# A planned order of work, laid out anew: the letter tables of a five-engine kernel

## The chip, the cores and the metric

The kernel runs on one core of a Trainium2 chip. A core has five engines with their own instruction queues: TensorE (PE in the profile, its weight loads PEld), VectorE (DVE), ScalarE (ACT), GpSimd (POOL) and SyncE (SP), which here issues all transfers between the device memory and the chip. The metric is the device time of one execution in microseconds; the kernel before took 2635.39 us as the median of three runs (2631.88 to 2636.12).

## The reference, cut to what matters

Four residual layers act on x of shape (8, 256, 64, 64), eight images of 256 channels. Each first normalises over 32 groups of channels:

```python
x = x + _L0_conv_ref(_gn(x), ...)   # three 7x7 gates over pooled (max, mean) planes, mixed by a softmax
x = x + _L1_conv_ref(_gn(x), ...)   # a 3x3 convolution, its weight mixed with block-circulant projections of itself
x = x + _L2_conv_ref(_gn(x), ...)   # a squeeze and excitation over channels (8-tap pairs folded into a weighted mean)
x = x + _L3_conv_ref(_gn(x), ...)   # shifted 8x8 window attention, 8 heads, with a relative bias and a mask
```

## The kernel before, in words

**Two lines of work.** Each image passes through a chain of named steps, the list FRONT (L508): `norm0a` to `norm0c` (group statistics of the first layer), `reduce0` to `reduce15` (channel maxima and means: TensorE turns two pairs of rows a step, L1986, VectorE takes their maxima, L1531), `zpool`, `hwconv` to `bandturn` (the three gates), `hwmean0` to `hwmean7`, `logits`, `mix`, `mixturn` (their mixture), `gate0` to `gate17` (the gated image, two matmuls a step on TensorE, L2058 and L2060, one product and one statistic on VectorE, L1624 and L1457), `norm1a` to `norm1c`, `lift0` to `lift3`, `conv0.0` to `conv23.1` (the convolution in a transformed form, 24 outputs of 18 matmuls, L2088) and `convend`. Beside it run streams of other work, one letter for each: on all engines `Y` is the setup of the weights in the first image and `E` the excitation; the attention of the image before, in 64 rows of windows, is `K` (tokens), `Q` (projections on TensorE, six matmuls of 512 columns each or twelve of 256, L2147, L2154 and L2163, and their evacuations on ScalarE), `S` (scores and maxima), `X` (exponentials), `T` (sums on VectorE, L1862 and L1864; turned probabilities on TensorE, L2189), `N` (normalisation on GpSimd), `W` on TensorE (the weighted values, L2208), `O` (heads) and `A` (the result added to the row on VectorE, L1871). For the image itself VectorE has `C` (statistics, L1727), `U` (maxima over rows and columns, L1742 and L1749), `B` and `J` (lower half of the convolution's inputs, and joined rows), `V` (row sums, L1713 and L1716); GpSimd has `R` (row and column sums), `D` (differences) and `W` (weighed rows, L902); SP has `Z` and `F` (store an image, fetch the next), `L` and `S` (load and store a row) and `G` (constants again).

**What sets the order.** An engine runs its queue in order. The queue is written out from tables: FIRST for the first image, TURN for each of the seven others, LAST_ROWS for the rows after the last image. An entry gives, for an engine and a step of the chain, the letters that are issued behind the engine's own part of that step (M). AHEAD names how many letters of a kind the first image has already done for the second; they are skipped there. The tables do not change what is computed, nor which semaphore an instruction waits for: an instruction that is issued too early stands in the queue and holds what is behind it.

```python
ahead, at_img = dict(AHEAD[engine]), 0
for kind, img, name in MAIN:
    ...
    yield "M"
    for letter in (TURN if at_img else FIRST)[engine].get(name, ""):
        if at_img == 1 and ahead.get(letter, 0):
            ahead[letter] -= 1
        else:
            yield letter
yield from LAST_ROWS[engine]
```

**Places that the prediction touches.** In the setup VectorE finds each partition's peak of the attention's weights (L1356 to L1358), GpSimd reduces them over partitions (L791 and L792), and VectorE scales by them (L1361 to L1369); each of the three is one `Y` of its engine. `norm0b` on VectorE writes the variance (L1446), GpSimd raises it to the power -1/2, `norm0c` on VectorE writes the shift (L1453), and ScalarE then normalises the first quarter of the image (L1082), for which `reduce0` on TensorE waits. A projection `p` (L2163) is added to the row by `A`; the next projection's bank is free when that is done. On SP the 64 transfers of the bias table (L671) are the last `Y`; the step `hwgate` has one transfer there (L689) and `hwrows` three (L693).

Of the kernel before, what the change touches and what calls it, by code (L numbers as in the profile page):

```python
# [7 lines left out]
NB, C, H, W = 8, 256, 64, 64  # L8
# [57 lines left out]
    "DVE": {"load": "YYUCUCCCCUCUCUCUCCCUCCUCYYYYYYYCC", "norm0a": "Y", "norm0b": "YYYY", "norm0c": "YYY",  # L66
# [7 lines left out]
        "convend": "JJJVCVVVVVVVCEUCUCCCUYUUUCEYAUACEEECCCCECECCEE"},  # L74
    "PE": {"reduce10": "Y", "reduce15": "Y", "zpool": "Y", "hwmean2": "Y", "hwmean5": "Y", "gate11": "Y",
        "gate17": "Y", "convend": "EYEEEEE"},
# [2234 lines left out]
```

How the kernel before makes its waits and increments, by code:

```python
            def link(self, ins):  # L444
                self.n += 1
                ins.then_inc(self.s, 1)
                self.eng.wait_ge(self.s, self.n)
# [88 lines left out]
        def wait_read(eng, name):  # L536
            if name in ADDED:
                eng.wait_ge(p_added, ADDED.index(name) + 1)
            elif name in BY_DVE:
                eng.wait_ge(v_taken, BY_DVE.index(name) + 1)
            else:
                eng.wait_ge(qp_read, BY_ACT.index(name) + 1)
# [75 lines left out]
                def load():  # L619
                    sp.dma_start(al[:, 0, :], dram(alphas, 0, [[0, P], [1, 5]])).then_inc(al_in, 16)
                    for u in range(UNITS):
                        half, co, ty, px = unit(u)
                        sp.dma_start(X[:, co, px], x[0, P * co:P * co + P, px]).then_inc(x_in[u], 16)
                    for dst, src in small:
                        sp.dma_start(dst, src).then_inc(consts_in, 16)
                    for g in range(P // BMAX):
                        sp.dma_start(WB[g::P // BMAX, :].rearrange("p (r n) -> p r n", r=BMAX),
                                     dram(w_conv, g * 2 * BMAX * TAPS, [[BMAX * C * TAPS, BMAX], [C * TAPS, BMAX],
                                                                        [1, 2 * BMAX * TAPS]])).then_inc(wconv_in, 16)
                    sp.wait_ge(zero_set, 1)
                    sp.dma_start(scratch_t[:, :], zeros).then_inc(zero_out, 16)
                    yield "load"
```

## Time and profile before

| | |
|---|---|
| median of three runs | 2635.39 us |
| profiled execution, its own time | 2639.28 us |
| its span | 2637.5 us |
| PE busy | 2268.7 us, 86% |
| DVE busy | 2210.3 us, 84% |
| ACT busy | 1550.4 us, 59% |
| POOL busy | 1445.6 us, 55% |
| mean granted TensorE clock | 0.956 |

A granted clock of 1.00 is 2.4 GHz and of 0.50 is 1.2 GHz. Busy time of PE counts matmuls from start to modelled end, so that one that stands alone counts longer than its share of a stream. Letters have no row of their own in the profile: a letter is found by the line that it issues. The convolutions of the eight images lie at 199.7, 490.1, 796.5, 1096.9, 1398.5, 1701.3, 2004.4 and 2307.1 us; the image that begins at 1264.8 us stands for the six between the second and the last, which are alike.

### The profile page before, as it was taken

What the parts mean: (1) busy time and instruction counts of PE and PEld (TensorE: products, weight loads), DVE (VectorE), ACT (ScalarE), POOL (GpSimd) and SP (SyncE); (2) the same over time, 40 slices, a digit from 0 to 9 for tenths busy, and PEclk for the clock granted to TensorE, in tenths of its full rate; (3) what the DMA queues carried; (4) which work ended last, traced back from release to release, by engine and by line L of the source; (5) the groups of instructions that cost most, each with busy time, mean ns of one, the idle gap of its engine ahead of it and who ended that gap; (6) DMA issues with size and microseconds to landing.
All of it is one profiled execution on the core that took longest, in us unless ns stands there. A gap on an engine that the chain in (4) does not pass through costs nothing. (4 is left out here: it accounts for less than half of the span.)

```text
span 2637.5 us, 67221 instructions
## 1 busy us (share of the span) xinstructions
PE 2268.7 (86%) x27686; PEld 1345.1 (51%) x27686; DVE 2210.3 (84%) x3721; ACT 1550.4 (59%) x3574; POOL 1445.6 (55%) x1150
## 2 busy tenths in 40 slices
PE   0558669898989989899989989899898989899897
PEld 0423346454745556455654557455664556545554
DVE  8988958888887988889898898879888888878665
ACT  1222046656765577645775567755766567755775
POOL 4315643466645583457735584466834676456455
PEclk9869879998999999999999999999999999999999
DMA  5400501022310231023311231104311223101221
GB/s 161 141 2 17 182 3 43 25 89 81 98 42 34 97 113 50 26 73 105 90 38 44 97 114 42 34 33 136 90 42 34 81 89 98 34 33 49 66 66 42
DMA packets 126065, 180.36 MB, mean 68 GB/s; under 512 B 72624, under 2 KB 114368, under 8 KB 115648
## 3 DMA queue, kind: packets, MB, share of 16 engines
q1 hardware_dynamic: 125760, 176.07, 21.3%
q8 instruction: 219, 3.59, 0.6%
q14 instruction: 86, 0.70, 0.1%
HBM read 103.15 MB, written 72.86 MB: 67 GB/s over the span
## 5 line engine op out<-in xcount | busy, mean ns | idle before, releaser
L2088 PE MATMUL F<-g_raw,cw_hi 128*128 128x512 f16 x2304 | 695.8, 384 | 17.5 <-DVE X L1497 8.7
L917 POOL TENSOR_TENSOR xs<-xs,rec 128x512 f32<-128x512 f32 x256 | 290.9, 1151 | 535.8 <-DVE rec L1864 534.5
L1206 ACT ACTIVATE xs<-xs,mx 128x64 f32<-128x64 f32 x1792 | 444.5, 334 | 40.3 <-DVE mx L1854 39.9
L2088 PE MATMUL F<-g_raw,cw_lo 128*128 128x512 f16 x1152 | 441.6, 383 | 0.0
L2088 PEld LDWEIGHTS F<-g_raw,cw_hi 128*128 128x128 f16 x2304 | 222.3, 98 | 282.3 <-issue 15.0
L1211 ACT ACTIVATE xs<-PTR 128x512 f32<-128x512 f32 x256 | 151.1, 590 | 214.8 <-PE PTR L2189 214.7
L902 POOL TENSOR_TENSOR tmp<-X,uw 128x512 f32<-128x512 f32 x128 | 175.9, 1391 | 130.7 <-DVE X L1699 93.4
L932 POOL TENSOR_TENSOR ot_lo<-ot,ot_hi 128x512 f16<-128x512 f32 x128 | 148.8, 1184 | 176.2 <-ACT ot_hi L1225 174.5
L1843 DVE TENSOR_TENSOR xs<-SP,bias 128x1024 f32<-128x1024 f32 (+2 forms) x192 | 159.8, 860 | 96.1 <-PE SP L2179 55.3
L1426 DVE SCALAR_TENSOR_TENSOR g_raw<-l0c,gn,g_raw 128x512 f16<-128x512 f32 x192 | 179.0, 975 | 51.6 <-ACT g_raw L1064 35.6
L2147 PE MATMUL QP<-tok_hi,qkv_hi 128*128 128x512 f16 x470 | 180.7, 385 | 34.6 <-ACT qq L1187 14.4
L1187 ACT ACTIVATE qq<-QP,q_bias,q_scale 128x512 f32<-128x512 f32 x118 | 91.6, 776 | 178.7 <-PE QP L2147 178.6
L1862 DVE TENSOR_REDUCE sums<-xs 128x16 f32<-128x1024 f32 x128 | 154.9, 1210 | 45.2 <-ACT xs L1201 24.1
L2088 PEld LDWEIGHTS F<-g_raw,cw_lo 128*128 128x128 f16 x1152 | 113.2, 98 | 141.0 <-issue 4.0
L2147 PE MATMUL QP<-tok_lo,qkv_hi 128*128 128x512 f16 x470 | 179.5, 382 | 0.0
L2189 PE MATMUL PTR<-ident,xs 128*128 128x128 f32 x1024 | 159.9, 279 | 22.8 <-ACT xs L1211 12.2
L2147 PE MATMUL QP<-tok_hi,qkv_lo 128*128 128x512 f16 x470 | 179.2, 381 | 0.0
L1986 PE MATMUL F<-ident,g_raw 128*128 128x129 f32 x1024 | 148.7, 290 | 35.0 <-ACT g_raw L1082 20.3
L1854 DVE TENSOR_REDUCE mx<-xs 128x16 f32<-128x1024 f32 x128 | 156.1, 1220 | 13.7
L2179 PE MATMUL SP<-kk,qq 32*64 32x64 f32 x8192 | 154.6, 224 | 11.2 <-issue 5.5
L1986 PEld LDWEIGHTS F<-ident,g_raw 128*128 128x128 f32 x1024 | 131.9, 198 | 55.6 <-DVE Z L1531 24.1
L2189 PEld LDWEIGHTS PTR<-ident,xs 128*128 128x128 f32 x1024 | 123.0, 143 | 68.7 <-POOL xs L917 31.9
(334 smaller groups left out, 5538.8 us busy)
## 6 DMA issues: line engine op xcount, KB each, us to landing
scratch_x<-X SPq DMA_DIRECT2D x32, 1024.0 KB, 4.8
xs<-scratch_x SPq DMA_DIRECT2D x56, 508.0 KB, 3.4
out_x<-xs SPq DMA_DIRECT2D x56, 508.0 KB, 2.8
X<-in_x SPq DMA_DIRECT2D x25, 1024.0 KB, 6.1
l0c<-scratch_t SPq DMA_DIRECT2D x8, 1876.0 KB, 9.0
l0c<-in_x SPq DMA_DIRECT2D x7, 1024.0 KB, 5.1
l0c<-scratch_t SPq DMA_DIRECT2D x8, 640.0 KB, 11.1
l0c<-scratch_t SPq DMA_DIRECT2D x8, 576.0 KB, 12.1
```

The source lines that it names most:

```text
L902: G.tensor_tensor(rows_view(tmp[:, 2 + m % 2, :]), rows_view(X[:, co, lo:lo + CHUNK]), uw[:, :].unsqueeze(1).to_broadcast([P, ROWS, W]), A ...
L917: G.tensor_tensor(keyed(sc[:, u % DEEP, :]), keyed(sc[:, u % DEEP, :]), rec[:, u % DEEP, :].unsqueeze(2).to_broadcast([P, 8, TOK]), ALU.mu ...
L1206: last = S.activation(keys, keys, ACT.Exp, bias=mx[:, u % DEEP, i:i + 1])
L1426: V.scalar_tensor_tensor(vin[:, slot(half, comp), 1, t, :, 1:1 + W], rows_view(src[:, t, :]), g_r[:, t:t + 1], vin[:, slot(half, comp), 0, ...
L1843: return V.tensor_tensor(windows(sc[:, buf:buf + 2, :])[:, :, w0:w1_, :], windows(SP[:, :, :])[:, :, w0:w1_, :], bias[:, kind, :, :, :].re ...
L1854: V.tensor_reduce(mx[:, buf:buf + 2, :].rearrange("p a k -> p (a k)"), sc[:, buf:buf + 2, :].rearrange("p a (k m) -> p (a k) m", m=TOK), A ...
L1862: seq.link(V.tensor_reduce(both(sums), sc[:, buf:buf + 2, :].rearrange("p a (k m) -> p (a k) m", m=TOK), AX.X, ALU.add))
L1986: last = T.matmul(turned_pair(j)[:, t, :], Gn[:, t, P * j:P * j + P], ident_mean[:, :], start=True, stop=True)
L2088: last = T.matmul(F[:, n % 2, :], wgt[:, ci, C3 * comp + dx, P * co:P * co + P], win[which], start=(ci == 0 and dx == 0 and j == 0), stop= ...
L2147: last = T.matmul(out_bank, wgt[:, ci, P * oc:P * oc + P], tk[:, ci, :], start=(j == 0), stop=(j == 5))
L2179: last = T.matmul(SP[TOK * h2:TOK * h2 + TOK, hs, 256 * cg + TOK * w:256 * cg + TOK * w + TOK], qq[rows, cg, win], kk[rows, cg, win], star ...
L2189: last = T.transpose(PTR[:, P * b:P * b + P], sc[:, u % DEEP, P * b:P * b + P], ident[:, :])
```

## The change

All five tables are written anew; no other line differs. The order that they hold was worked out with TensorE's stretches at half clock counted in their account. The number of letters of each kind in TURN is the same before and after. In FIRST, VectorE does two `U` and two `A` less (AHEAD gives 6 in place of 8, and 2 in place of 4), and ScalarE one `K` less (AHEAD gives none in place of 1). Cut to the rows that are spoken of below:

```diff
 FIRST = {
-    "SP": {"load": "YYY", "band2": "Y", "hwmean2": "Z", "gate0": "ZFF", "gate2": "F", "gate14": "Z", "norm1a": "F",
-        "conv4.1": "Z", "conv10.0": "L", "conv22.0": "L", "conv23.1": "S", "convend": "GL"},
...
-        "reduce12": "RR", "reduce15": "R", "band2": "R", "lift2": "D", "lift3": "D", "conv0.1": "D", "conv1.0": "D",
-        "conv5.1": "D", "conv6.0": "YD", "conv7.0": "W", "conv9.0": "W", "conv9.1": "W", "conv11.0": "W",
...
-    "DVE": {"load": "YYUCUCCCCUCUCUCUCCCUCCUCYYYYYYYCC", "norm0a": "Y", "norm0b": "YYYY", "norm0c": "YYY",
...
-        "bandcopy": "YY", "logits": "YY", "mix": "YY", "mixturn": "Y", "gate16": "Y", "norm1c": "Y", "conv3.1": "BY",
-        "conv6.1": "BBY", "conv8.0": "JB", "conv8.1": "JJB", "conv10.1": "VVBB", "conv11.0": "VB", "conv11.1": "V",
...
-        "convend": "JJJVCVVVVVVVCEUCUCCCUYUUUCEYAUACEEECCCCECECCEE"},
...
+    "SP": {"norm0a": "Y", "reduce3": "Y", "reduce11": "Y", "reduce13": "Y", "hwmean1": "ZF", "gate2": "Z",
+        "gate4": "F", "gate9": "F", "gate11": "Z", "lift2": "F", "lift3": "Z", "conv22.1": "SL", "conv23.1": "G",
+        "convend": "LL"},
...
+        "reduce14": "R", "reduce15": "RRR", "zpool": "R", "lift3": "D", "conv1.1": "DD", "conv2.1": "D",
+        "conv4.0": "Y", "conv5.0": "DW", "conv6.1": "W", "conv7.1": "W", "conv9.0": "DW", "conv13.0": "W",
...
+    "DVE": {"load": "YYCCCCCCUUUCCUCUCCCUCUCCCYYYYYYY", "norm0a": "YYYYYYYY", "norm0c": "Y", "reduce0": "U",
...
+        "mixturn": "Y", "gate1": "Y", "lift1": "Y", "conv4.0": "BY", "conv4.1": "B", "conv5.1": "BB", "conv6.0": "J",
+        "conv6.1": "B", "conv8.0": "JBJ", "conv8.1": "V", "conv9.0": "V", "conv9.1": "Y", "conv10.1": "VVV",
...
+        "conv22.1": "CVVCVVUUV", "conv23.0": "V", "convend": "JJJVVVVVVVVUCUUEUUYUUECEEECECECCCCCEE"},
...
 TURN = {
...
-    "DVE": {"norm0a": "E", "norm0b": "TA", "norm0c": "KKAU", "reduce1": "T", "reduce2": "U", "reduce3": "U",
...
-        "mixturn": "ATKA", "gate1": "K", "gate4": "T", "gate9": "S", "gate15": "SAKK", "gate16": "ATT", "lift1": "S",
...
-    "PE": {"norm0b": "Q", "norm0c": "QTQ", "reduce2": "Q", "reduce3": "Q", "reduce5": "TQ", "reduce6": "STWT",
-        "reduce7": "SQW", "reduce8": "Q", "reduce11": "Q", "reduce12": "T", "reduce13": "QT", "reduce14": "Q",
-        "zpool": "Q", "hwconv": "Q", "hwgate": "WTQTQWS", "hwrows": "Q", "band0": "S", "band2": "Q", "bandturn": "Q",
-        "hwmean0": "T", "hwmean1": "Q", "hwmean2": "TQW", "hwmean3": "Q", "hwmean4": "T", "hwmean5": "Q",
-        "hwmean6": "T", "hwmean7": "QWS", "logits": "S", "mix": "Q", "mixturn": "Q", "gate0": "Q", "gate1": "T",
-        "gate3": "Q", "gate4": "QT", "gate6": "QT", "gate8": "Q", "gate10": "SQTW", "gate12": "S", "gate14": "W",
-        "gate15": "QQ", "gate16": "QQQ", "gate17": "T", "norm1a": "Q", "lift0": "TQ", "lift1": "TQST", "lift2": "WW",
-        "conv0.1": "QSQ", "conv1.0": "Q", "conv2.1": "T", "conv7.0": "QT", "conv8.0": "Q", "conv9.0": "QT",
-        "conv9.1": "Q", "conv10.0": "WS", "conv10.1": "TQ", "conv11.0": "WS", "conv11.1": "Q", "conv13.0": "Q",
-        "conv15.0": "Q", "conv16.0": "Q", "conv16.1": "Q", "conv17.0": "TQ", "conv17.1": "QT", "conv19.0": "T",
-        "conv19.1": "WSQT", "conv20.0": "WS", "conv20.1": "Q", "conv22.0": "Q", "conv23.0": "Q", "conv23.1": "TQ",
-        "convend": "TQWTQTQEWEQEESQESE"},
+    "DVE": {"norm0a": "E", "norm0b": "U", "norm0c": "TAKUK", "reduce0": "A", "reduce1": "U", "reduce2": "U",
...
+        "band1": "S", "band3": "TAK", "bandturn": "A", "hwmean0": "T", "logits": "S", "mix": "ST", "mixturn": "A",
+        "gate1": "KKA", "gate3": "T", "gate9": "S", "gate12": "S", "gate15": "AK", "gate16": "KATT", "lift1": "S",
...
+    "PE": {"norm0b": "Q", "norm0c": "Q", "reduce1": "Q", "reduce2": "Q", "reduce3": "T", "reduce4": "QT",
+        "reduce5": "Q", "reduce6": "WST", "reduce7": "TQSW", "reduce8": "Q", "reduce11": "Q", "reduce12": "T",
+        "reduce13": "QT", "reduce14": "Q", "reduce15": "Q", "hwgate": "QWTQTQWS", "hwrows": "Q", "band0": "S",
+        "band3": "Q", "bandturn": "TQ", "hwmean1": "TQ", "hwmean2": "WQ", "hwmean3": "Q", "hwmean5": "TQ",
+        "hwmean6": "T", "hwmean7": "QWS", "logits": "S", "mix": "Q", "mixturn": "Q", "gate1": "QT", "gate3": "Q",
+        "gate5": "QT", "gate6": "Q", "gate8": "Q", "gate9": "ST", "gate11": "WQT", "gate12": "SW", "gate14": "Q",
+        "gate15": "Q", "gate17": "QQQ", "norm1a": "Q", "norm1b": "TT", "lift0": "QW", "lift2": "T", "lift3": "TSW",
+        "conv0.0": "Q", "conv0.1": "QSQ", "conv1.1": "Q", "conv2.1": "T", "conv6.1": "QT", "conv7.0": "Q",
+        "conv7.1": "Q", "conv9.0": "Q", "conv9.1": "TQTWS", "conv10.1": "WS", "conv12.0": "Q", "conv13.1": "Q",
+        "conv15.1": "Q", "conv16.1": "TQ", "conv17.0": "T", "conv17.1": "Q", "conv18.0": "TQ", "conv18.1": "Q",
+        "conv19.1": "WSQT", "conv20.0": "WS", "conv20.1": "Q", "conv22.0": "Q", "conv22.1": "Q", "conv23.1": "TQTQ",
+        "convend": "TQTWQEWEQEESQESE"},
...
-AHEAD = {"SP": {}, "POOL": {"N": 4, "O": 1, "R": 22}, "ACT": {"K": 1, "O": 1, "T": 4, "X": 2}, "DVE": {"A": 4, "E": 1, "T": 2, "U": 8}, "PE": {"Q": 2, "T": 4, "W": 2}}
+AHEAD = {"SP": {}, "POOL": {"N": 4, "O": 1, "R": 22}, "ACT": {"O": 1, "T": 4, "X": 2}, "DVE": {"A": 2, "E": 1, "T": 2, "U": 6}, "PE": {"Q": 2, "T": 4, "W": 2}}
...
```

## Rows read from the trace of the kernel before

**Rows 1.** One stretch: from:to, us, busy PE, PEld, DVE, ACT, POOL, clock, DMA.
```profile
199.70:306.80 107.10, 99.41 (x432) 42.97 (x432) 91.89 (x118) 22.47 (x35) 60.85 (x41) 0.96 0.17 59
```

**Rows 2.** Stretches of the image that begins at 1264.8 us.
```profile
1264.80:1350.60 85.80, 81.71 (x1292) 60.87 (x1291) 75.17 (x149) 64.68 (x151) 47.23 (x43) 0.98 0.27 80
1350.60:1398.50 47.90, 39.58 (x619) 21.49 (x619) 43.81 (x72) 34.29 (x87) 22.74 (x18) 1.00 0.15 46
1398.50:1533.90 135.40, 132.32 (x1190) 67.57 (x1187) 115.95 (x145) 73.64 (x178) 79.50 (x57) 1.00 0.19 63
1533.90:1566.80 32.90, 23.01 (x363) 14.54 (x362) 28.21 (x75) 23.05 (x55) 25.88 (x22) 0.90 0.33 103
```

**Rows 3.** TensorE in order of time around 1534 us: start, length, engine, line.
```profile
1533.73 0.60 PE L2189 MATMUL PTR<-ident,xs 128*128 128x128 f32 x4
1534.17 0.38 PE L2147 MATMUL QP<-tok_hi,qkv_hi 128*128 128x512 f16 x1
...
1535.46 0.60 PE L2189 MATMUL PTR<-ident,xs 128*128 128x128 f32 x4
```

**Rows 4.** VectorE in order of time around norm0.
```profile
1558.22 1.21 DVE L1862 TENSOR_REDUCE sums<-xs 128x16 f32<-128x1024 f32 x1
...
1560.68 0.75 DVE L1871 SCALAR_TENSOR_TENSOR xs<-QP,wm,xs 128x512 f32<-128x512 f32 x1 [0.90 <-PE QP L2163]
1561.35 0.15 DVE L1453 SCALAR_TENSOR_TENSOR gn<-F,gn 128x2 f32<-128x2 f32 x1
1561.42 3.33 DVE L1828 TENSOR_TENSOR tok_lo<-tok,tok_hi 128x512 f16<-128x512 f32 x2
...
1565.33 1.94 DVE L1749 TENSOR_REDUCE Z<-X 128x32 f32<-128x1024 f32 x1
```

**Rows 5.** TensorE in order of time around norm0.
```profile
1557.92 0.59 PE L2163 MATMUL QP<-ot_hi,wo_hi 128*128 128x512 f16 x1
...
1565.46 0.39 PE L2147 MATMUL QP<-tok_hi,qkv_hi 128*128 128x512 f16 x1 [2.07 <-DVE xs L1871]
...
1566.77 0.94 PE L1986 MATMUL F<-ident,g_raw 128*128 128x129 f32 x7
```

**Rows 6.** ScalarE in order of time around norm0.
```profile
1560.56 0.63 ACT L1172 ACTIVATE tok_hi<-tok 128x512 f16<-128x512 f32 x1
1561.54 2.38 ACT L1082 ACTIVATE g_raw<-X,gn 128x1024 f32<-128x1024 f32 x2 [0.34 <-DVE gn L1453]
```

**Rows 7.** GpSimd in order of time around norm0.
```profile
1559.09 0.70 POOL L836 TENSOR_TENSOR gn<-gn,neg_half 128x2 f32<-128x2 f32 x1
```

**Rows 8.** Stretches at half clock in two images.
```profile
1553.80:1560.60 6.80, 3.71 (x10) 1.66 (x10) 4.96 (x21) 6.10 (x21) 6.41 (x7) 0.50 0.00 0
1857.60:1867.80 10.20, 7.33 (x20) 3.29 (x20) 7.87 (x25) 9.14 (x24) 9.73 (x10) 0.50 0.00 0
```

**Rows 9.** GpSimd, VectorE and TensorE in order of time, first convolution.
```profile
239.21 0.41 POOL L791 PARTITION_ALL_REDUCE gm<-gm  x1 [5.85 <-issue]
...
240.00 0.15 DVE L1361 TENSOR_SCALAR gm<-gm 128x1 f32<-128x1 f32 x1 [4.36 <-POOL wm L792]
...
242.14 0.61 PE L2088 MATMUL F<-g_raw,cw_hi 128*128 128x512 f16 x2 [3.52 <-DVE X L1497]
```

**Rows 10.** SP in order of time, first image.
```profile
97.20 0.43 SPq L666 DMA_DIRECT2D ot<-in_w_qkv  x1
121.18 0.53 SPq L689 DMA_DIRECT2D tmp<-in_c_rows  x1
...
127.17 23.32 SPq L671 DMA_DIRECT2D tok_hi<-in_rel_t  x64
```

**Rows 11.** VectorE in order of time, between the first two images.
```profile
342.05 0.16 DVE L1774 SCALAR_TENSOR_TENSOR part<-F,part 128x2 f32<-128x2 f32 x1 [8.10 <-POOL part L912]
```

**Rows 12.** TensorE in order of time, second image's first steps.
```profile
356.60 0.61 PE L2147 MATMUL QP<-tok_hi,qkv_hi 128*128 128x512 f16 x1 [2.42 <-DVE tok_lo L1828]
...
359.13 4.86 PE L1986 MATMUL F<-ident,g_raw 128*128 128x129 f32 x24
```

More of the change, by code:

```diff
@@ L53 @@
 FIRST = {
[12 rows of a table removed]
-    "DVE": {"load": "YYUCUCCCCUCUCUCUCCCUCCUCYYYYYYYCC", "norm0a": "Y", "norm0b": "YYYY", "norm0c": "YYY",
[7 rows of a table removed]
-        "convend": "JJJVCVVVVVVVCEUCUCCCUYUUUCEYAUACEEECCCCECECCEE"},
-    "PE": {"reduce10": "Y", "reduce15": "Y", "zpool": "Y", "hwmean2": "Y", "hwmean5": "Y", "gate11": "Y",
-        "gate17": "Y", "convend": "EYEEEEE"},
[8 rows of a table added]
+        "convend": "WWRRRRRRRRRRRRRRRRERRRRRR"},
[14 rows of a table added]
 }
 TURN = {
[33 rows of a table removed]
-        "conv23.1": "KACV", "convend": "JJJVVVVVVVVECECEECESECESE"},
[11 rows of a table removed]
-        "convend": "TQWTQTQEWEQEESQESE"},
[23 rows of a table added]
+        "conv23.1": "XKXTQTQ", "convend": "TQKTQOEQQXX"},
[10 rows of a table added]
+        "convend": "JJJCVVVVVVVVECECEECESECESE"},
[11 rows of a table added]
+        "convend": "TQTWQEWEQEESQESE"},
 }
-AHEAD = {"SP": {}, "POOL": {"N": 4, "O": 1, "R": 22}, "ACT": {"K": 1, "O": 1, "T": 4, "X": 2}, "DVE": {"A": 4, "E": 1, "T": 2, "U": 8}, "PE": {"Q": 2, "T": 4, "W": 2}}
+AHEAD = {"SP": {}, "POOL": {"N": 4, "O": 1, "R": 22}, "ACT": {"O": 1, "T": 4, "X": 2}, "DVE": {"A": 2, "E": 1, "T": 2, "U": 6}, "PE": {"Q": 2, "T": 4, "W": 2}}
 LAST_ROWS = {
-    "SP": "SLSLSLSLSLLSSS",
-    "POOL": "ENNNNXOXXXNNNNXXOXNXNNNXXOXXNNNNXXOXNXNNNXXXONNXNNXXOXNXNNNXXNOXNXNNXXXXNNONNO",
-    "ACT": ("KKXXQTQTQQTKTKOKKXKXQQXXQQTTTKTOXXKKQXTXKQQTQTTKKOKXXXQQXKTQQTKTTKOXKXKXQQXTQQTTKTXOXKKXKTQQXTKQQTTO"
-          "XKXKQQXXQQTTTKXTXKOKKKQXQTXQQTTXXTXOXTKTTTO"),
-    "DVE": "EAKAKTTSPSKPKAATTSPSTKPKAATSKPPSKATATSPPKSKATATSSPTKPKAATSPPSKAKTATSTSPKPKAATSSTTTPAPASAA",
-    "PE": ("QQQQTQTQTWSTQWSQQQQQQQTQTSTWTWSQQQTQQQQTQTSTQWWSQQQQQTQTQTSTQWWSQQQQQTQTSWTSTWQQQQTQQQTQQTSTWWQSQQQQ"
-          "QQTSTTTSWWQQTQQQQQQTSWSTTWQTQTQTQTWWQQ"),
+    "SP": "SLSLSLSLSLSSSL",
+    "POOL": "ENNNNXOXXXNNNNXXOXXNNNNXXOXXNNNNXOXXXNNNNXXXONXNNNOXXXNXNNNXXNOXNXNNXXXXNNONNO",
+    "ACT": ("XKKTXQKTQQTQTKOKKXXQXQXKQTQTTTKXOKKXKKXQQXQTTQTTKOXXKKQXQXTQQTTKTKOKXXXQKQXQTQKTTTXXOKKXTXQQKQTQTKTK"
+          "OKXXXKQQQXQTTKTTXXOKKQXQXQTQTTXXTXOXTTKTTKO"),
+    "DVE": "AETAKKTSPSKPKAATTSPSKPKAATTSKPSPKATATSKPPSKATATSSTPPKKAATSKPPSKAATTSTPSKPKAATSSTPTTPAAASA",
+    "PE": ("QQTTQQQTQWTSQWSQQQQQQTQTSQTTWWSQQQQQQTQTQTSTQWWSQQQQQTQTQTSTQWWSQQQQQTQTSWTSTQWQQQTQQQTQTQTSQWWSQQQQ"
+          "QQTSTTWTQWSQTQQQQQQTSTWSQTWTQTQTQTWWQQ"),
 }
```

87 rows, old and new, of tables (FIRST, TURN) are left out of this document.

## The prediction

> **What bounds the kernel now.** I read the page's busy shares first. TensorE is busy 86% of the span and VectorE 84%, so neither bounds the whole, and the bound has to be found stage by stage. A table of busy time by stretch was therefore the second view. In the first image the convolution lasts 107.1 us with TensorE busy 99.41 us of it [rows 1]. Six images of some 302 us follow that are alike, and the one that begins at 1264.8 us falls into four stages [rows 2]: up to `mixturn` 85.8 us (TensorE 81.71, VectorE 75.17), the gated image 47.9 us (VectorE 43.81, TensorE 39.58), the convolution 135.4 us (TensorE 132.32, VectorE 115.95), and from its end to the next `reduce0` 32.9 us, in which nobody is full (VectorE 28.21, TensorE 23.01, clock 0.90). The reader is to see four bounds: TensorE in the first and the third stage, VectorE in the second, and a chain of waits in the fourth. A letter moved from one stage to another is worth something only by what bounds the two.
>
> The third view was the order of time around `norm0`, where the clock drops. The clock is at 0.50 for 6.8 us in one image and for 10.2 us in the next, under the same order [rows 8]. Before both, TensorE had long idle times: in the stretches shown it is busy 3.71 of 6.8 us and 7.33 of 10.2.
>
> **The change part by part.** All sums go against the profiled execution, 2639.28 us, 3.9 us above the median.
>
> *Prices.* A projection `Q` costs TensorE 1.29 us at full clock, from 1534.17 to the next group at 1535.46, and a `T` 0.44 us, from 1533.73 to 1534.17 [rows 3]. At half clock a projection that starts at 1557.92 lets VectorE go on at 1560.68, 2.76 us later [rows 4, 5]. On VectorE a `T` takes 1.56 us: it starts at 1558.22, and the wait of 0.90 us that follows it begins at 1559.78 [rows 4]. A `U` takes up to 1.94 us [rows 4].
>
> *norm0, in six boundaries.* VectorE now does `TA` behind the variance and the shift only then. `A` waits 0.90 us for the half-clock projection, so the shift comes at 1561.35 [rows 4], though GpSimd had the power ready at 1559.09 + 0.70 = 1559.79 [rows 7]. In the new table one `U` stands there: from 1558.22 it ends at 1560.16, and the shift is 1.2 us earlier. ScalarE is then still busy with tokens until 1561.19, so its normalisation starts not at 1561.54 but at 1561.2 at best [rows 6]: 0.3 us. More lies behind it. On TensorE two projections stand ahead of `reduce0`; the second is held 2.07 us by an `A` that VectorE does only after two `K` of 3.33 us, and `reduce0` starts at 1566.77, when its data have lain since 1561.54 + 2.38 = 1563.92 [rows 4 to 6]. The new table leaves one `Q` behind `norm0c` and has the other at `reduce1`. `reduce0` could then start at about 1563.7: −3.1 us. That is not all kept. From the end of the convolution to `norm0c` TensorE has two `Q` and two `T` less, of which one `Q` and one `T` come into the stage up to `mixturn`, which is full: 1.29 + 0.44 = +1.7 us. Sum −1.4 us an image. Bounds: 0, if the stage behind takes all of it back, and −2.9, if the 85.80 − 81.71 = 4.1 us of idle there hide all but a little.
>
> *The gated image, seven times.* VectorE bounds this stage and has one `T` less there (it now stands at `mix`): up to −1.5 us. TensorE has one `Q` less, which counts only where VectorE waits for it. I take −1.3, with 0 (the step waits for other engines) and −1.5 as ends. The `T` at `mix` lies in a stage where VectorE idles 85.80 − 75.17 = 10.6 us; if that cover is gone, it costs its 1.56 us there.
>
> *The convolution, seven times.* TensorE has two `Q` and one `T` more: 2 × 1.29 + 0.44 = +3.0 us in a stage with 135.40 − 132.32 = 3.1 us of idle [rows 2]. Much of this idle is the matmuls' waits for their inputs, which a letter fills only if it stands at the right place; I take +2.2, between 0 (all filled) and +3.0 (none). On VectorE one `C` leaves the stage, and 19 us of idle there cover the rest.
>
> *The first image's convolution.* VectorE stands 4.36 us until 240.00 for GpSimd's reduction over partitions, which GpSimd itself starts late (its 5.85 us idle with no releaser), and TensorE then stands 3.52 us until 242.14 [rows 9]. The new tables have VectorE's peaks and GpSimd's reduction at `conv4.0`, and the scales only at `conv9.1`, so the stall should go: −3.5. Ends: −4.4 (VectorE's whole stall) and +2, if the reduction now waits for VectorE's peaks and holds GpSimd's differences `D`, which stand behind it at `conv5.0`: no row shows that wait, and I bound it by half of today's 4.36.
>
> *Into the second image.* There a projection of six half-clock matmuls runs from 356.60 to 359.13, ahead of `reduce0` [rows 12]. It moves to `reduce1`. It ran while data were still on their way in part, so I take half, −1.3, between 0 and −2.5. Two `U` of up to 1.94 us come into this image's first steps on VectorE, where it waits for TensorE. Six `C` that leave `convend` gain nothing: VectorE stands 8.10 us there for GpSimd's excitation [rows 11], and GpSimd's letters ahead of that are not fewer.
>
> *At nothing.* The 64 transfers of the bias table take 23.32 us of SP's queue; they move ahead of the transfers of `hwgate` and `hwrows`, into a queue that issues nothing between 97.6 and 121.18 us [rows 10]; late by a little, they cost up to 2 us. The setup's reordering around `norm0a` lies beside weights that VectorE prepares anyway: 0, ±2. The fetches and `G` on SP, moved by some steps, lie beside a convolution of 135.4 us [rows 2]; if a fetch is late once, the longest wait in these rows, 8.10 us, bounds it [rows 11]. The rows after the last image have the same letters in a new order: 0, ±3.
>
> *Sum.* −3.5 − 1.3 + 6 × (−1.4) + 7 × (−1.3) + 7 × 2.2 = −3.5 − 1.3 − 8.4 − 9.1 + 15.4 = −6.9 us: 2639.3 becomes 2632.4 profiled, and on the median's scale 2635.4 − 6.9 = **2628 us**. With all lower ends the sum is −4.4 − 2.5 − 17.4 − 10.5 + 0 − 3, with the setup's −2 = −40; with all upper ends it is 2 + 0 + 0 + 0 + 21 + 2 + 2 + 3 = +30, and one late fetch more makes +38.
>
> The half-clock stretches differ by 3.4 us between images of one order [rows 8], about as much as the plan means to win at one boundary. The Trainium skill, "TensorE: Matmul & The Clock Gate", Part 1 (The HAM clock gate), says that how many matmuls run cold differs between runs of the same kernel. This speaks against any order built on fixed stretches, and the trace agrees so far as 6.8 and 10.2 us go; by that rule the −8.4 of the six boundaries may come to half or to nothing, the first rival below.
>
> **The rivals.**
>
> *No change, about 2634.* The stretches at half clock fall elsewhere under the new order, and a boundary gains in some images and loses in others. Then half of the six boundaries' −8.4 is kept (−4.2), the gated image keeps −9.1, the convolution costs its upper +3.0 (+21, less a third that the idle takes, +14), and the first image gives −4.8 only in part (−3): −2. For it: the 3.4 us above. Against it: `reduce0` waits at all six boundaries for the same `A`, at whichever clock.
>
> *Slower, about 2651.* The convolution is TensorE's, 132.32 of 135.40 us [rows 2]. If all 3.0 us come on top, seven images cost 21 us, and if neither the boundary nor the gated image gives anything back, because VectorE's letters set the pace there (43.81 of 47.9 us) and their whole count is the same, only the first image's −4.8 stands against it: +16. It decides from about 1.5 us an image that isn't given back. For it: the convolution is the one stage where a TensorE letter certainly costs. Against it: the letters are taken from stages in which TensorE was on the path too.
>
> *A larger gain, about 2600.* The idle of TensorE at each boundary, 32.9 − 23.01 = 9.9 us, shrinks by 5 and the idle in the convolution takes the added letters: 6 × (−5) − 5 = −35. For it: the 2.07 us wait and the half-clock projection are both in the chain. Against it: the sums of statistics and the excitation in that stage are a chain on VectorE and GpSimd, and it is not made shorter.
>
> *The order does not do what it says*, in that its half-clock stretches are as long as before: this changes no letter's place, and leads to the first rival's time.
>
> **How the numbers follow.** Chances: forecast 0.42, larger gain 0.08, no change 0.25, slower 0.25. A measurement of this kernel can tell 0.2%, about 5.3 us, from no change. The forecast at 2628 (−7) and the larger gain lie beyond it: faster 0.50. Within it: 0.25, slower 0.25. The forecast's own range, with the convolution between +1 and +2.7 an image and the boundary between −2.5 and −1, is 2618 to 2636. The range to hold the time 8 times in 10 reaches below to 2606, short of the larger gain's middle, and above to 2650, to the slower rival's middle: about 0.07 lies below and 0.13 above.
>
> **What would show it.** Right: at the six boundaries `reduce0` starts within some 2 us of its data, with no `A` wait of 2 us before a projection; the convolutions are 137 to 138 us long; the gated image is 46 to 47 us; and the first convolution shows no stall of VectorE near 240 us. Wrong in one step each: `reduce0` still 2.5 us behind its data; a convolution of 138.4 us or more, with TensorE's idle unchanged (slower); a stage up to `mixturn` longer by more than the 1.7 us. The whole is wrong if the period between `reduce0`s, 302 us, isn't shorter by about half a microsecond to one, or if the time moves in the setup or the rows at the end, which I cost at nothing.

## The result, and the profile after

The changed kernel takes 2619.17 us in the median of four runs (2613.57 to 2621.74), against 2635.76 us before: a ratio of 0.9931, 95% interval 0.9918 to 0.9945. That is −16.6 us where −7 were forecast, with the time inside the range. The profiled execution took 2613.57 us and the one of before 2639.28 us, so the two traces differ by 25.7 us: 3.5 us of that is how far the old trace lies over its median, and 5.6 how far the new one lies under its own.

The first view is the busy time by stretch, as in [rows 1, 2]: the first image's convolution, then the four stages of the image that begins at 950.60 us, whose period of 297.1 us is among the shorter ones (296.1 to 300.6). Columns are from:to, us, busy PE, PEld, DVE, ACT, POOL, granted clock, DMA share, GB/s. The program's lines are one further down than before.

```profile
203.70:303.00 99.30, 96.87 (x433) 42.42 (x434) 86.87 (x119) 19.91 (x31) 56.76 (x40) 0.98 0.19 64
950.60:1037.30 86.70, 82.98 (x1302) 61.52 (x1301) 76.82 (x152) 65.89 (x159) 50.31 (x47) 0.98 0.15 45
1037.30:1084.10 46.80, 37.75 (x606) 20.50 (x606) 42.72 (x71) 34.83 (x87) 21.36 (x17) 1.00 0.15 47
1084.10:1217.70 133.60, 133.37 (x1209) 68.79 (x1199) 116.98 (x144) 74.16 (x179) 81.73 (x57) 1.00 0.27 88
1217.70:1247.70 30.00, 21.03 (x353) 13.55 (x351) 26.61 (x75) 20.90 (x47) 23.67 (x21) 0.89 0.30 106
```

The row to see is the convolution: 133.60 us with TensorE busy 133.37. Before it was 135.40 with 132.32 [rows 2]. TensorE has 1.05 us more work in it and 2.85 us less idle time, so the stage with the added letters got shorter. What TensorE waited for there stands in the view of waits (engine, what, for whom: us in total, times, longest), first before, in the convolution from 1398.5 us:

```profile
PE O L2208 <- issue: 1.5, 1, 1.5
PE QP L2163 <- ACT vv L1194: 1.4, 1, 1.4
PE F L2088 <- DVE X L1497: 0.2, 1, 0.2
```

and in the changed kernel, in the one from 1084.1 us:

```profile
PE F L2089 <- DVE X L1498: 0.2, 1, 0.2
```

Of 3.1 us of waits, 2.9 belonged to two letters of the attention (a projection `Q` and a `W`) and only 0.2 to the convolution's own matmuls. Both big waits are gone. Over the seven convolutions the projection's wait for ScalarE is there in each before (0.8 to 1.4 us) and in one after (0.3 us).

Stage by stage the two traces add up so (image 0 is the first):

| part | before, us | after, us | difference | predicted |
|---|---|---|---|---|
| load to the second image's `reduce0` | 359.1 | 353.9 | −5.2 | −4.8 |
| `reduce0` to the gated image, images 1 to 7, sum | 603.4 | 607.7 | +4.3 | +10.2 |
| convolution's end to `reduce0`, six boundaries, sum | 195.6 | 184.2 | −11.4 | −18.6 |
| gated image, seven, sum | 334.1 | 330.5 | −3.7 | −9.1 |
| convolutions, seven, sum | 948.8 | 936.0 | −12.8 | +15.4 |
| last convolution's end to VectorE's last instruction | 192.9 | 195.9 | +3.0 | 0 |

(The predicted −3.1 at a boundary and +1.7 behind it are shown apart here, six times each. The first row flatters the change: one projection that stood ahead of the second image's `reduce0` now stands behind it, and that image's stage from `reduce0` to the gated image is 2.5 us longer, which the second row counts.)

At the boundary, in order of time around 1241 us (start, length, engine, line; the bracket is the wait before it), the new order looks so:

```profile
1241.80 1.91 DVE L1750 TENSOR_REDUCE Z<-X 128x32 f32<-128x1024 f32 x1
1244.11 0.16 DVE L1454 SCALAR_TENSOR_TENSOR gn<-F,gn 128x2 f32<-128x2 f32 x1 [0.40 <-POOL gn L837]
...
1244.69 2.36 ACT L1083 ACTIVATE g_raw<-X,gn 128x1024 f32<-128x1024 f32 x2
...
1243.38 0.70 POOL L837 TENSOR_TENSOR gn<-gn,neg_half 128x2 f32<-128x2 f32 x1
...
1246.42 0.39 PE L2164 MATMUL QP<-ot_hi,wo_hi 128*128 128x512 f16 x1 [2.18 <-DVE xs L1872]
...
1247.72 1.05 PE L1987 MATMUL F<-ident,g_raw 128*128 128x129 f32 x8
```

From the first letter behind the variance to the shift it is 2.31 us now (1241.80 to 1244.11) and was 3.13 [rows 4]: the `U` fills VectorE's wait, but GpSimd gives the power 2.28 us after that point (1243.38 + 0.70) in place of 1.57 [rows 4, 7]. `reduce0` starts 0.67 us behind its data (1244.69 + 2.36 = 1247.05), where it was 2.85 behind [rows 5, 6]. At the six boundaries `reduce0` starts 0.24 to 1.48 us behind its data, where it was 2.49 to 2.97. Yet a wait for VectorE's addition is still there at all six, of 1.75 to 2.18 us, only in front of the one projection that stayed.

In the first convolution the stall of VectorE is gone as foreseen [rows 9]; GpSimd reduces at 232.61, and VectorE's scales run at 245.96 with no wait. The second image's `reduce0` has no projection ahead of it [rows 12]:

```profile
232.61 0.42 POOL L792 PARTITION_ALL_REDUCE gm<-gm  x1 [5.73 <-issue]
...
245.96 0.14 DVE L1362 TENSOR_SCALAR gm<-gm 128x1 f32<-128x1 f32 x1
...
203.73 1.01 PE L2089 MATMUL F<-g_raw,cw_hi 128*128 128x512 f16 x2 [12.92 <-DVE cw_lo L1353]
...
353.89 2.33 PE L1987 MATMUL F<-ident,g_raw 128*128 128x129 f32 x9 [3.62 <-ACT g_raw L1083]
```

The third of these rows shows what the table hides: TensorE now stands 12.92 us before the first convolution for the weights that VectorE prepares (6.62 us for other data before), so of the 7.9 us by which that convolution is shorter, 6.0 are given back in the gated image ahead of it. Of these 7.9 us, 2.5 are TensorE's own work, which ran at a mean clock of 0.98 in place of 0.96 (99.41 to 96.87 us). The load is 5.8 us longer and the reduction 7.7 shorter in the same way.

### The profile page after: what moved, and what is told of

It reads as the page before. It is cut to its first block, busy times and chain, and to the rows that moved or that the text cites. A ratio compares the mean times of both kernels' runs of the same rounds, so it can differ in the third digit from the quotient of the medians.

```text
span 2611.8 us, 67227 instructions
## 1 busy us (share of the span) xinstructions
PE 2249.4 (86%) x27686; PEld 1342.5 (51%) x27686; DVE 2213.0 (85%) x3721; ACT 1548.9 (59%) x3574; POOL 1461.5 (56%) x1150
## 4 chain that ended last, share of the span: by engine, by line
PE 47%; DVE 21%; POOL 8%; ACT 7%; issue 5%; DMA 0%; DVEq 0%; POOLq 0%; SPq 0%; ACTq 0%
PE F L2089 23%; PE QP L2148 5%; POOL tmp L963 4%; PE QP L2155 3%; PE SP L2180 3%; ACT xs L1207 3%; PE PTR L2190 2%; PE O L2209 2%; PE F L1987 2%; PE QP L2164 2%; DVE sums L1863 2%; DVE xs L1844 1%; DVE mx L1855 1%; DVE raw L1572 1%; DVE stats L1458 1%
## 5 line engine op out<-in xcount | busy, mean ns | idle before, releaser
L903 POOL TENSOR_TENSOR tmp<-X,uw 128x512 f32<-128x512 f32 x128 | 168.8, 1336 | 122.5 <-DVE X L1700 119.2
L1427 DVE SCALAR_TENSOR_TENSOR g_raw<-l0c,gn,g_raw 128x512 f16<-128x512 f32 x192 | 159.4, 872 | 48.5 <-ACT g_raw L1065 38.5
L1191 ACT ACTIVATE kk<-QP,bq,gm 128x512 f32<-128x512 f32 x117 | 90.8, 776 | 144.2 <-PE QP L2148 144.0
L1987 PEld LDWEIGHTS F<-ident,g_raw 128*128 128x128 f32 x1024 | 133.5, 199 | 59.5 <-ACT g_raw L1083 31.7
```

Of the source, the lines that this page charges most:

```text
L903: G.tensor_tensor(rows_view(tmp[:, 2 + m % 2, :]), rows_view(X[:, co, lo:lo + CHUNK]), uw[:, :].unsqueeze(1).to_broadcast([P, ROWS, W]), A ...
L1427: V.scalar_tensor_tensor(vin[:, slot(half, comp), 1, t, :, 1:1 + W], rows_view(src[:, t, :]), g_r[:, t:t + 1], vin[:, slot(half, comp), 0, ...
L1987: last = T.matmul(turned_pair(j)[:, t, :], Gn[:, t, P * j:P * j + P], ident_mean[:, :], start=True, stop=True)
```

## The experiments

All ratios are to the kernel before, run on the same chip beside it; e1 to e4 shared one chip, e5 and a1 to a3 another, a0 and a4 to a6 a third.

| kernel | ratio | 95% interval | median, us |
|---|---|---|---|
| e1, new TURN alone | 0.9948 | 0.9929 to 0.9967 | 2620.6 |
| e2, norm0 alone | 1.0051 | 1.0031 to 1.0070 | 2648.4 |
| e3, one projection later | 1.0008 | 0.9996 to 1.0020 | 2637.6 |
| e4, SP's row alone | 0.9988 | 0.9976 to 1.0001 | 2632.8 |
| e5, new FIRST alone | 0.9987 | 0.9976 to 0.9997 | 2634.5 |
| a1, changed, old norm0 | 1.0013 | 0.9998 to 1.0027 | 2640.6 |
| a2, changed, TensorE kept busy | 1.0019 | 1.0006 to 1.0032 | 2643.0 |
| a3, changed, one more projection moved | 0.9982 | 0.9971 to 0.9994 | 2634.0 |
| a0, changed, again | 0.9945 | 0.9930 to 0.9961 | 2621.6 |
| a4, changed, old LAST_ROWS | 0.9947 | 0.9933 to 0.9960 | 2620.2 |
| a5, changed, old start of the convolution | 0.9933 | 0.9918 to 0.9948 | 2620.3 |
| a6, changed, one shift of 1.7 us | 0.9978 | 0.9967 to 0.9989 | 2628.9 |

**e1: which table holds the gain.** Before with the new TURN; FIRST, AHEAD and LAST_ROWS old.

> Before, with the new TURN alone; FIRST, AHEAD and LAST_ROWS are the old ones. Theory 1 (the first image gives a good quarter of the gain): in the profiles the first image and the way into the second are 5.2 us shorter and the rows at the end 3.0 us longer, so TURN alone would be worth 25.7 - 5.2 + 3.0 = 23.5 us between the two profiled runs, and about 14 us between medians, of which the six boundaries hold about 11, the seven gated images 4 and the convolutions 14, less some 4 in the stage up to mixturn. Theory 2 (the periods are shorter only because the first image hands over another state): under 5 us.

TURN alone gives −0.52%, nearly all of it, as theory 1 said. Its seven convolutions last 133.5 to 134.0 us, like the changed kernel's. But its periods come in two kinds: 296.0, 297.1 and 297.2 us, and 303.7, 303.9 and 303.5. Five of these periods (all but the 296.0 us of the second image) are one order, so the difference isn't the order's: the two short ones of 297 us hold 10.2 us at half clock, the three long ones 20.5 to 27.3. Two reductions of it, by stretch:

```profile
958.20:1044.90 86.70, 83.03 (x1302) 61.57 (x1300) 76.84 (x152) 65.68 (x159) 50.34 (x47) 0.98 0.16 45
1559.20:1648.20 89.00, 85.95 (x1302) 64.45 (x1300) 76.00 (x150) 64.60 (x158) 49.84 (x46) 0.94 0.15 44
```

The same 1302 matmuls take TensorE 2.92 us more in the second, at a mean clock of 0.94 in place of 0.98.

**e2: the boundary alone, in the old order.**

```diff
 TURN DVE
-"norm0b": "TA", "norm0c": "KKAU"
+"norm0b": "U", "norm0c": "TAKKA"
 TURN PE
-"norm0c": "QTQ"
+"norm0c": "Q", "reduce1": "TQ"
 TURN ACT
-"norm0b": "KK"
+"norm0c": "KK"
```

> Before, with the edits at norm0 alone: VectorE norm0b U and norm0c TAKKA in place of TA and KKAU, TensorE norm0c Q and reduce1 TQ in place of QTQ and nothing, ScalarE's KK behind norm0c in place of norm0b. Theory 1 (the boundary's chain was what held reduce0): from the convolution's end to reduce0 some 2.5 us less in each of six boundaries (32.6 becomes about 30), of which the projection and the turn that are moved into the stage behind take back 1.7 there: net -0.5 to -1.5 each, -3 to -9 us in all. Rival: the stage up to mixturn has 4 us of idle and takes them in, and all 2.5 are kept: -15 us. Second rival: the shift is late anyway, since GpSimd is still at its sums when the variance comes: under 1 us each.

The boundaries are 30.8 us long (one 31.0), 1.8 us less. The stage behind is 87.0 to 90.0 us long and was 83.0 to 88.1, which is more than was won (+18 us over seven against −11 over six), and the kernel is 0.5% slower; none of the three expected outcomes came. In the view by stretch, the stage up to `mixturn`, and the boundary behind that image:

```profile
1267.50:1355.60 88.10, 82.35 (x1303) 60.98 (x1302) 75.97 (x149) 64.97 (x153) 50.31 (x46) 1.00 0.27 80
1539.00:1570.00 31.00, 22.33 (x353) 13.90 (x352) 26.36 (x74) 22.48 (x54) 22.16 (x19) 0.81 0.32 104
```

This stage ran at full clock with 0.64 us more work on TensorE than in [rows 2], and yet lasts 2.3 us more: its idle time grew from 4.1 to 5.75 us. So the prediction's +1.7 for this stage is not a ceiling. Letters that arrive there make others wait.

**a1: the like edit undone in the new order.**

```diff
 TURN DVE
-"norm0b": "U", "norm0c": "TAKUK", "reduce0": "A", "reduce1": "U"
+"norm0b": "TA", "norm0c": "KKAU", "reduce1": "UU"
 TURN PE
-"norm0c": "Q", "reduce1": "Q"
+"norm0c": "QQ"
 TURN ACT
-"norm0c": "KK"
+"norm0b": "KK"
```

> The changed kernel with the old order at norm0: VectorE TA and KKAU, then UU at reduce1, TensorE QQ at norm0c and nothing at reduce1, ScalarE KK at norm0b. Theory 1 (what a boundary gains is taken back by the stage up to mixturn, as when norm0 alone was changed and the six images after it were no shorter): the boundaries are 2 us longer, the stage behind 1 to 2 us shorter, and the median is within 3 us of the changed kernel's 2619. Rival (in the new order the stage behind has room, and the boundary's 2.4 us are kept): +12 to +15 us, about 2632.

The rival came true. The shortest boundaries are 31.8 us against 30.0, the six in sum 199.1 against 184.2, and the stage behind is not shorter for it (607.4 us over seven against 607.7):

```profile
1226.40:1258.20 31.80, 22.48 (x359) 14.02 (x358) 27.89 (x76) 22.46 (x48) 25.47 (x21) 0.89 0.30 106
1258.20:1345.20 87.00, 80.80 (x1296) 59.80 (x1295) 77.05 (x151) 65.04 (x159) 48.49 (x46) 1.00 0.15 43
```

From 0.993 or 0.9945 the ratio rises to 1.0013, some 18 to 22 us. Between the traces, 18.7 us apart, the boundaries hold 14.9: 1.8 us at each of six make 11, and the rest lies at the three longest. The runs of this kernel scatter with the clock: their mean clock is 0.944 to 0.956, with 2648 us at the lowest and 2632 to 2636 at 0.953 to 0.956. Nearly the same edit is worth nothing, or less, in one order and all it gives at the boundary in the other. What in the new order makes the room was not isolated.

**e3 and a5: the wait of 1.4 us in the convolution.** e3 moves the waiting projection one step back in the old order; a5 puts the projections at the start of the new order's convolution back.

```diff
 e3, TURN PE
-"conv0.1": "QSQ", "conv1.0": "Q"
+"conv0.1": "QS", "conv1.0": "QQ"
 a5, TURN PE
-"lift3": "TSW", "conv0.0": "Q", "conv1.1": "Q"
+"lift3": "TSWQ", "conv1.0": "Q"
```

> Before, with one letter moved on TensorE: conv0.1 QS and conv1.0 QQ in place of QSQ and Q, so that the projection that stood 0.8 to 1.4 us for ScalarE's evacuation in each of seven convolutions comes one step later. Theory 1 (the convolution is TensorE's, and its idle time is added to it in full): each convolution 0.8 to 1.4 us shorter, -8 us in all, 0.3% under before. Rival (the idle is made up elsewhere, since the convolution's end waits for VectorE and GpSimd as well): the gap goes, the convolution keeps its 135 us, and the time is within 2 us of before.

> The changed kernel with TensorE's projections at the start of the convolution where they were: one back from conv0.0 to lift3 and one from conv1.1 to conv1.0, so that the last of QSQ at conv0.1 is early again. Theory 1 (in before this projection stood 0.8 to 1.4 us for ScalarE's evacuation behind its exponentials, and the new place took that stall out of every convolution): the gap before it is back with 0.8 us or more, and the convolutions become 134.5 to 135 us long in place of 133.6, +5 to +9 us in all. Rival (the stall went because ScalarE's own letters moved): no gap, 133.6 us as in the changed kernel, and the time within 2 us of it.

In e3 the wait did not go but change hands. In the convolution from 1700.8 us the projection now waits for VectorE's addition, and a matmul of the convolution for its input:

```profile
PE QP L2164 <- DVE xs L1872: 0.9, 1, 0.9
PE SP L2180 <- issue: 0.8, 1, 0.8
PE F L2089 <- DVE X L1498: 0.6, 1, 0.6
PE QP L2155 <- ACT vv L1195: 0.2, 1, 0.2
```

0.9 + 0.6 is as much as the 1.4 that went: the rival's idle time made up elsewhere is the nearer picture, and theory 1 failed. In a5 the wait for ScalarE's values did not come back at all: 132.06 us of work in convolutions of 132.3 us, one projection (1.3 us) less than in the changed kernel, and the time is that of the changed kernel. So TensorE's places at the start of the convolution are not what took the wait out; the rival names ScalarE's own letters, which the runs do not isolate.

**e4: transfers and the other wait.** SP's row of the new TURN in the old kernel.

> Before, with SP's row of the new TURN alone. In before, two image transfers of 1 MB are issued 0.6 us apart late in the convolution, the DMA share is 0.9 to 1.05 while they last, and TensorE stands 1.2 to 1.7 us at conv19 or conv20 in five of seven images with no releaser. Theory 1 (the stall is code that comes late past the transfers): with the transfers apart the stall goes, and the convolutions of these images are 1.2 to 1.7 us shorter, some -7 us in all. Rival (the stall belongs to the place in the code and not to the transfers): the stall stays at the same letters, and the time is within 2 us of before. Second rival: the transfers now collide with other code, and stalls of the same kind come up at another step.

In the kernel before, SP issues two image transfers of 1 MB within 0.6 us at 597, 904, 1204, 1505, 1808 and 2112 us, and TensorE stands still 7 to 9 us after each, for 1.70, 0.40, 1.25, 1.47, 1.30 and 1.53 us, with no releaser. One of these, SP's rows and then TensorE's:

```profile
1505.46 0.34 SPq L718 DMA_DIRECT2D X<-in_x  x1
1506.02 0.33 SPq L704 DMA_DIRECT2D scratch_x<-X  x1
...
1514.33 0.73 PE L2208 MATMUL O<-xs,vv 64*32 64x64 f32 x50 [1.47 <-issue]
```

In e4 the wait is gone from five of these six convolutions, which last 134.0 to 134.3 us (the sixth has one of 1.4 us at another letter, and 134.7). Its seven convolutions take 939.0 us in sum against 948.8 before and 936.0 in the changed kernel; this much of the convolution's gain is shown to be SP's. It was paid for at the boundary, which takes 32.2 to 36.1 us (204.4 us over six against 195.6): in the longest of them VectorE's statistics wait for an image transfer, which is later now.

```profile
1541.94 0.69 DVE L1728 BATCH_NORM_STATS2 stats<-X 128x6 f32<-128x512 f32 x1 [1.36 <-DMA X<-in_x]
```

The time is no different (−0.12%; theory 1 had some −7 us). The rival of a fixed place in the code is out, since the wait moved with SP's row. That the wait is code arriving late is supported by the traces' transfer records, which name a queue `instruction` (q8, packets of 16 KB). In the wait until 1514.33 such a packet lies from 1512.04 to 1512.98. In all 14 traces together TensorE has 101 waits of 0.4 us or more with no releaser between 300 and 2450 us, and each of them ends 1.2 to 1.7 us after a packet of that queue has ended; a moment taken at random does so in 4 of 100 cases. That the image transfers delay the packet is not shown. The changed kernel has twelve such pairs from its second image on and only two waits of this kind over 0.5 us behind them (1.45 us at 930.0, 0.69 at 1529.3), and 8 of the 14 waits in the kernel before follow no pair.

**e5 and a4: the first image and the last rows.**

> Before, with the new FIRST and AHEAD alone; TURN and LAST_ROWS are the old ones. Theory 1 (the prediction's: VectorE's stall of 4.36 us for GpSimd's reduction goes, and TensorE's 3.52 us with it): the first image's convolution 3.5 us or more shorter, and the second image's first reduce0 up to 5 us earlier, so -3 to -5 us in all. Rival (the work of the setup is only moved ahead of the gates: in the changed kernel the load is 5.8 us longer, the reduction 7.7 shorter, the gated image 6.0 longer and the convolution 7.9 shorter): the sum stays near -1 us or the second image pays for it.

> The changed kernel once more, on the same chip as the three below, for a ratio that theirs can be set against. Expected 0.993 of before, as in its first runs (0.9918 to 0.9945).

> The changed kernel with the old LAST_ROWS. In the profiles so far the rows after the last convolution take 189.8 to 194.3 us with the old list and 195.0 to 199.4 with the new one. Theory 1 (the new list is slower by what these stages show): 2 to 4 us under the changed kernel on the same chip, and so under both kernels. Rival (the new list fits the new TURN, which leaves the engines in another order behind the last convolution, and the old list fits it worse): 0 to 3 us over it.

FIRST alone gives −0.13%, 3.4 us with an interval from 0.8 to 6.3, as theory 1 had it; in its trace the second image's `reduce0` is 3.2 us earlier (359.1 to 355.9), and its convolution begins 1.8 us earlier. With the old LAST_ROWS no difference is seen: 0.9947 against 0.9945 on the same chip, and 194.4 us behind the last convolution against 195.4. At most 1.0 of the 3.0 us in the table above is the list's by these two traces; the two ratios, each uncertain by some 4 us, can't exclude 3.

**a2, a3 and a6: what the half clock has to do with it.** a2 adds 12 matmuls in TensorE's idle time before norm0's mean; a3 moves the last projection from `norm0c` to `reduce0`; a6 adds 8 matmuls once, in the second image.

```diff
 a2, TURN PE (H issues T.matmul(QP, wo_hi, qkv_hi[0:512]) 12 times into the free bank)
-"convend": "TQTWQEWEQEESQESE"
+"convend": "TQTWQEWEQEESQESEH"
 a3, TURN PE
-"norm0c": "Q"
+"reduce0": "Q"
 a6, TURN PE (H issues 8 of these the first time, then none)
-"reduce8": "Q"
+"reduce8": "HQ"
```

> The changed kernel with 12 extra matmuls of 512 columns (2.6 us at full clock) on TensorE at the end of convend, where it stands idle for 3.4 us before norm0's group mean; they write the free projection bank, which the next projection writes over. Theory 1 (the periods have two lengths, 297 and 303 us, by how much of norm0 and of the reduction runs at half clock): the half-clock stretch at norm0 is gone or under 4 us, the long periods become rare, and the median is 3 to 8 us under the changed kernel's 2619, with less scatter. Rival (VectorE's chain sets the boundary at either clock): the stretch goes and the time stays within 2 us. Second rival (the extra matmuls run at half clock, take 5 us and hold the group mean): each boundary 2 us longer, +12 us.

> The changed kernel with TensorE's second projection at the boundary moved from norm0c to reduce0, so that the first pairs of rows are turned as soon as ScalarE has normalised them and not behind that projection, which waits 1.7 to 2.2 us for VectorE's addition. Theory 1 (reduce0 is held by the projection): reduce0 1.5 us earlier at each boundary; if TensorE's idle there is what counts, the stage behind keeps 1 us of it: -6 us. Rival (the stage up to mixturn is full on TensorE and the projection's 1.3 us come back there): reduce0 is earlier, mixturn is not, and the time is within 2 us of 2619.

> The changed kernel with 8 matmuls of 512 columns (1.7 us) added once, at reduce8 of the second image, on TensorE; they write the free projection bank. Theory 1 (the later periods are 297 or 303 us long by where the half-clock stretches fall, and a shift of 1.7 us in the second image deals them anew): the time differs from the changed kernel by more than 1.7 us, 3 to 12 us more if the new order met a favourable place. Rival (the lengths follow the order alone): +0 to +2 us, and the periods behind the second image are as in the changed kernel.

In a2 the 6.8 us at half clock that lie at the boundary are gone at four of six boundaries, and 3.4 us come later, on `reduce0`. Boundary, half-clock stretch and reduction of one image:

```profile
1227.80:1258.10 30.30, 22.26 (x364) 14.06 (x363) 26.91 (x75) 21.49 (x48) 23.97 (x21) 0.99 0.30 106
1257.40:1260.80 3.40, 3.40 (x16) 3.06 (x15) 2.60 (x5) 3.40 (x10) 3.32 (x3) 0.51 0.00 0
1258.10:1347.60 89.50, 84.39 (x1302) 63.04 (x1301) 77.75 (x152) 65.19 (x158) 50.01 (x47) 0.97 0.15 44
```

At the boundary nothing was won: at 0.99 and with the 12 matmuls the stage lasts 30.3 us, at 0.89 and without them it lasted 30.0. Whether half clock costs nothing there, or the matmuls took back what it gave, this run doesn't separate. On the reduction, where TensorE is busy all 3.40 us, it costs: the stage lasts 89.5 us in place of 86.7. The same is seen without any edit in a0, in two reductions of one execution and one order, the first with 3.4 us more at half clock at its start:

```profile
1551.00:1640.50 89.50, 84.68 (x1302) 63.15 (x1300) 77.18 (x152) 65.61 (x159) 50.24 (x47) 0.96 0.15 43
1851.00:1937.70 86.70, 83.03 (x1302) 61.58 (x1301) 76.83 (x152) 65.50 (x159) 50.35 (x47) 0.98 0.16 45
```

a2 is 0.7 to 0.9% slower than the changed kernel, which none of its three expectations had; 12.2 us of the 26.6 between the traces lie in the reductions, and 3.5 behind the last convolution, which takes 199.4 us there with the letter at its head. a3 fails in the same way, 0.4 to 0.5% over the changed kernel: four of its six boundaries are 29.4 us, but the reductions behind them 89 to 90.5 us long, with the projection's 1.3 us in them and some 3.4 us at half clock at their start, in all six.

a6 is the plainest. 1.7 us of work, once, cost 7 to 9 us against a0 on the same chip: 7.3 between the medians, 0.33% or 8.7 us between the ratios, with some 5 us to either side. Its second image is as long as a0's (296.3 and 296.1 us); the five behind it, whose order is the same, last 305.3, 298.7, 302.8, 300.0 and 298.9 us against 300.3, 297.1, 304.0, 300.0 and 297.1. The first of the five, in a6 and in a0:

```profile
651.60:956.90 305.30, 279.67 (x3456) 167.17 (x3455) 264.44 (x440) 196.36 (x471) 178.24 (x139) 0.96 0.21 69
649.70:949.90 300.20, 277.16 (x3456) 165.66 (x3455) 263.27 (x439) 195.03 (x470) 176.97 (x138) 0.98 0.22 70
```

Over the five, a6 has 85 us at half clock and a0 61, and TensorE is busy 6 us longer for the same work, of 7.3 us that the five last longer. Theory 1 stands: part of the changed kernel's time is where the half-clock stretches fall.

## Why the prediction was right, and where it was not

The direction was right and the time lay in the range, but the sum did not come out: −6.9 was added up, −25.7 lies between the traces and −16.6 between the medians. The convolution alone was wrong by 28 us, and that the time still lay in the range is in part luck: the boundaries, the gated images and the rows at the end gave 15.6 us less than forecast and hid over half of it.

- *First image and the way into the second*, −4.8: measured −5.2 in the trace, of which 2.5 come back in the second image's next stage, and −3.4 in e5. The stall that was named is gone, and TensorE's wait of 3.52 us with it. But the setup's reordering, costed at 0 ± 2, moved 6 to 8 us to and fro between stages, which only happen to cancel.
- *norm0 and the stage behind it*, −1.4 an image: in the trace −11.4 at six boundaries and +4.3 in the seven stages behind, −1.0 to −1.3 an image. The size was right; its mechanism was so in part. The sentence that `reduce0` waits at all six boundaries for the same `A` was read off one of them: in the trace before, the 2.07 us wait is there only at the boundary of [rows 5], with its 6.8 us at half clock. At the other five, with 10.2 us, the first of the two projections ran at half clock and the second followed with no such wait, and `reduce0` lay 2.49 to 2.97 us behind its data all the same. In the changed kernel the one projection left waits 1.75 to 2.18 us at all six. I overlooked that ScalarE's `KK` moves behind `norm0c`, and GpSimd was later than I took it. e2 shows that the step was not safe: the like edit in the old order costs 0.5%.
- *The gated image*, −1.3 each: −0.5 on average. Five of the seven are 0.75 to 1.2 us shorter; one is 0.9 longer with a wait of TensorE of 1.72 us until 1383.0 that has no releaser, and one is as long as before with 2.9 us at half clock.
- *The convolution*, +2.2 each: this is the step that failed, in sign; it measured −1.8 on average, 28 us over seven images. Two mistakes made it. The letters of `conv23.1` stand behind the last matmul, so one `Q` and one `T` of the three added letters belong to the boundary; the true addition is one `Q`, and TensorE's busy time in the stage grew by 1.05 us, not 3.0. And I wrote that much of the 3.1 us of idle time was matmuls waiting for their inputs, without reading the waits: 2.9 of it was two letters, one behind ScalarE's evacuation and one in the stop that follows a pair of transfers.
- *The rows at the end*, 0 ± 3: within what a4 can tell.
- *The rival of no change* rested on the half-clock stretches falling elsewhere. Its mechanism is real (a6, a2), and it has a size: within one kernel the runs at a mean clock of 0.961 take 2627 to 2632 us and those at 0.954 2638 to 2642, before. The changed kernel is not faster by less half clock. Its runs stand at 0.950 to 0.958, those of before at 0.953 to 0.961, and its trace holds 227 us at half clock against 234 before. The Trainium skill, "TensorE: Matmul & The Clock Gate", Part 1 (The HAM clock gate), says that the number of matmuls that run cold varies between runs of one kernel. The changed kernel's 2615.4 us at 0.957 and 2627.9 at 0.950, on one chip, agree; [rows 8] shows two images of one run and not two runs.
- *The slower rival* took all of TensorE's added work as time. It failed for the convolution's reason.
- *The larger gain*, about 2600, let the idle of TensorE take the letters added to the convolution. In that it was nearer than the forecast; its 5 us less at each boundary measured 1.9.
- *The forecast's own range*, 2618 to 2636, does not follow from its terms: with the convolution at +1 or +2.7 and the boundary at −2.5 or −1 the sum runs from 2613 to 2634.
- *What would show it*: `reduce0` within 2 us of its data, a gated image of 46 to 47 us (five of seven) and the missing stall came as written; the convolutions of 137 to 138 us and the boundary without the wait did not.

What stays open: which of the rows of TURN lets the boundary's gain be kept in the new order (a1) and lost in the old (e2), whether ScalarE's row alone takes the wait of 1.4 us out of the convolution, and what delays the code.

## What to carry to other kernels

Before a stage is called full, read who its few idle microseconds wait for: 2.9 us of waits of two letters, not of the stage's own work, helped to decide here whether more letters cost or gained. An order is one thing: single rows of a better one (e2, e3, e4) were worth nothing or less in the old one, and one undone row (a1) took the whole gain back. Where the clock falls in steps, time a change by several runs and read the mean clock beside each, because a shift of 1.7 us moved the whole by 7 to 9.

## What the runs showed of the hardware

- A stretch at half clock costs where TensorE is busy in it: on a full reduction 3.4 us more of it, in one execution of one order, made the same 1302 matmuls take 84.68 us in place of 83.03, and the stage was 2.8 us longer (a0). At the boundary, where TensorE is busy 3.75 of 6.8 us in the changed kernel, taking the stretch away with 12 matmuls won nothing (a2).
- Work put into the idle time to keep the clock up took the 6.8 us stretch away and left one of 3.4 us some 10 us later, on the busy stage, at four of six boundaries (a2).
- Two transfers of 1 MB issued within 0.6 us were followed 7 to 9 us later by 0.4 to 1.7 us in which TensorE issued nothing and waited for nothing that the profile shows, at each of six pairs in one order and at two of twelve in another.
- In 14 traces all 101 waits of TensorE of 0.4 us or more with no releaser, between 300 and 2450 us, ended 1.2 to 1.7 us after a 16 KB packet on the queue named `instruction` had ended.
